# Softmax sums turned into columns for a small reciprocal, and spread from a line in memory

## The chip, the core and the metric

The kernel runs on one core of a Trainium2 chip. The metric is device time in microseconds, the median of several executions of the whole program: one launch that reads the input and the weights from memory and writes the output back.

## The reference

Two attention layers follow each other on four images of 64 channels and 32 x 32 = 1024 positions. Each layer is a group norm, three projections, softmax attention over the 1024 positions, an output projection and a residual.

```python
def layer(x):                                  # twice, with other weights
    h = group_norm(x, 32 groups, w, b)         # per image, two channels to a group
    q, k, v = h @ Wq + bq, h @ Wk + bk, h @ Wv + bv
    attn = softmax(q @ k.T * 64 ** -0.5)       # 1024 x 1024 per image
    return x + (attn @ v) @ Wo + bo
```

The change concerns the softmax's denominators: for each image and layer 1024 sums, whose reciprocals scale the 64 x 1024 result.

## The kernel before

An image of a layer is a unit; there are eight, 0 to 3 for the first layer and 4 to 7 for the second. The 64 channels of one half of the positions lie in partitions 0 to 63, those of the other half in partitions 64 to 127, so a unit's data are tiles of 128 x 512.

Each engine has its own list of instructions, written out by hand in the order in which it runs them; engines meet through semaphores alone. Three units are in work at once. In turn w of the loop (`for w in range(2, LAST)`, turn 1 written out ahead of it in the same manner) TensorE computes the scores of unit w in eight tiles, multiplies the exponentials with the values of units w-1 and w, and computes scores of unit w+1 for their row maxima, in eight steps that share one PSUM tile, `ps_max`; it also projects q and k of unit w+2 into the bank `ps_scores[0]`, from which tile 6 of the scores has to wait until the projections are read. The other engines follow:

- ACT takes the eight exponentials of unit w, `exp(w, t)`, and copies and norms for the units around it.
- DVE reduces each maximum step, `part(w + 1, m)`, joins the eight, `join`, then makes the low parts of q and k of unit w+2 (`low_front`, `low_back`, from `ps_scores[0]`). Ahead of that it works out the group norm's statistics (`own_stats` to `affine`) of unit w+2; `affine` needs a reciprocal root from POOL.
- POOL takes that root, `root(w + 2)`, first, then adds up the exponentials of unit w in six steps; after the fourth it finishes unit w-1, `finish`: it multiplies the attention result with the spread reciprocals `rden` and adds the residual.
- SP issues most DMAs, in order: the spreading of the reciprocals of unit w-1, the swaps of unit w+2 (`cross`, the halves exchanged), the row of maxima of unit w+1 (`place_rows`), and results.

The denominators of unit w-1 come from TensorE in turn w (`denominators`): 256 columns in each partition, every quarter of the 128 partitions holding 256 of the 1024 sums, each repeated in all 32 rows of its quarter. DVE takes reciprocals of this 128 x 256 tile in two halves, `reciprocal(w - 1, 0)` and `(w - 1, 1)`, between two maxima. Eight DMAs of 32 rows each, six from SP and two from ACT, place them into `rden`, 128 x 512. The last two units finish partly on DVE (`finish_tail`).

Of the kernel before, what the change touches and what calls it, by code (L numbers as in the profile page):

```python
# [6 lines left out]
ACT = mybir.ActivationFunctionType  # L7
# [4 lines left out]
P = 128  # L12
C = P // 2
# [17 lines left out]
def attention_pair(nc, x, layer_params, consts, out):  # L31
# [20 lines left out]
    with ExitStack() as ctx:  # L52
# [47 lines left out]
        pick = sb("pick", [P, 4 * C])  # L100
        quarter_rden = sb("quarter_rden", [P, HALF // 2])
        rden = sb("rden", [P, HALF])

# [59 lines left out]
        attn_copied = sem("attn_copied")  # L163
        quarter_done = sem("quarter_done")
        rden_in = sem("rden_in")
        last_spread = sem("last_spread")
# [27 lines left out]
        def back_hi_of(unit):  # L194
            return (back_hi, unit) if unit else (first_back_hi, 1)

        def pool_adds(unit):
            return POOL_ADDS if unit < LAST - 1 else TAIL_ADDS[unit - LAST + 1]
# [4 lines left out]
        def scores_buffer(unit, t):  # L203
            return ps_scores[t % 2] if unit < LAST else (ps_scores[0], ps_scores[1], ps_max)[t % 3]

        block = ctx.enter_context(nc.Block())

        @block.sync
        def _(sp):
# [19 lines left out]
            def place_rows(u):  # L229
# [3 lines left out]
                for n in range(2):  # L233
                    row = q_row[u % 2][n * C:n * C + 1, :].bitcast(F32).rearrange("p (t n) -> p t n", t=JS)
                    sp.dma_start(row, max_rows[n * JS:(n + 1) * JS, :].bitcast(F32)).then_inc(row_in[u % 2], 16)

            def spread_rden(u):
                sp.wait_ge(quarter_done, 2 * u + 2)
                if u == LAST - 1:
                    sp.wait_ge(tail_normed, 1)  # L240
                elif u:
                    sp.wait_ge(normed, u)
                for n in range(2):
                    for block in (2 * n, 2 * n + 1):
                        for c in range(1 if n and u < LAST - 1 else 2):
                            sp.dma_start(rden[quarter(block), c * HALF // 2:(c + 1) * HALF // 2],
                                         quarter_rden[quarter(2 * n + c), :]).then_inc(rden_in, 16)
# [17 lines left out]
            for w in range(UNITS):  # L265
                if w:
                    spread_rden(w - 1)
                if w + 2 < UNITS:
                    swap_hi(w + 2)
                    swap_lo(w + 2)  # L270
                if w + 1 < UNITS:
                    place_rows(w + 1)
                if w > B:
                    store(w - 1 - B)
# [4 lines left out]
        def _(pool):  # L279
# [35 lines left out]
            def finish(u):  # L315
                a = attn[u % 2]
                pool.wait_ge(rden_in, 128 * (u + 1))
                pool.wait_ge(attn_copied, u + 1)
# [25 lines left out]
        def _(act):  # L344
# [106 lines left out]

            def spread_rden(u):
                act.wait_ge(quarter_done, 2 * u + 2)
                if u:
                    act.wait_ge(normed, u)
                for block in (2, 3):
                    act.dma_start(rden[quarter(block), HALF // 2:HALF],
                                  quarter_rden[quarter(3), :]).then_inc(rden_in, 16)

# [17 lines left out]
            for w in range(UNITS):  # L477
# [11 lines left out]
                if prep:  # L489
                    apply_norm(w + 2)  # L490
                exp(w, 4)
                exp(w, 5)
                if prep:
                    high_front(w + 2)
                    high_back(w + 2)
                if 0 < w < LAST:
                    spread_rden(w - 1)
                if 0 < w < LAST:
# [15 lines left out]
        def _(dve):  # L514
# [99 lines left out]
            def first_add(u):  # L614
                dve.wait_ge(exp_done, TILES * u + 2)
                if u >= 2:
                    dve.wait_ge(den_mm, u - 1)
                dve.tensor_tensor(prob_sum[u % 2][:, :], probs[0][:, :], probs[1][:, :],
                                  ALU.add).then_inc(first_added, 1)

            def reciprocal(u, c):
                cols = slice(c * P, (c + 1) * P)
                sums = ps_misc[:, cols] if u < LAST else ps_max[:, HALF + c * P:HALF + (c + 1) * P]
                if c == 0:
                    dve.wait_ge(den_mm, u + 1)
                    if u:
                        dve.wait_ge(rden_in, 128 * u)
                dve.reciprocal(quarter_rden[:, cols], sums).then_inc(quarter_done, 1)  # L628
# [31 lines left out]
            def finish_tail(u):  # L660
                a, n = attn[u % 2], u - LAST + 3
                dve.wait_ge(rden_in, 128 * (u + 1))
                dve.wait_ge(attn_copied, u + 1)
# [61 lines left out]
            part(2, 4)  # L725
            reciprocal(0, 0)
            part(2, 5)
            reciprocal(0, 1)
            part(2, 6)
            part(2, 7)  # L730
            join(2, neg_max[:, :])
            low_front(3)
# [4 lines left out]
            for w in range(2, LAST):  # L737
# [13 lines left out]
                part(w + 1, 5)  # L751
                reciprocal(w - 1, 0)
                if not prep:
                    part(w + 1, 6)
                reciprocal(w - 1, 1)
                if prep:
                    part(w + 1, 6)
                part(w + 1, 7)
                join(w + 1, neg_max[:, :])
                if prep:  # L760
# [19 lines left out]
        def _(pe):  # L780
# [143 lines left out]
            def spread_last(c):  # L924
                if c == 0:
                    pe.wait_ge(pick_set, 4)
                pe.wait_ge(quarter_done, 2 * LAST + c + 1)
                for k in range(2):
# [110 lines left out]
            values(1, 3)  # L1039
            pe.wait_ge(quarter_done, 2)  # L1040
            turn_max(2)
# [11 lines left out]
            for w in range(2, LAST):  # L1053
# [34 lines left out]
                values(w, 3)  # L1088
                pe.wait_ge(quarter_done, 2 * w)
                turn_max(w + 1)  # L1090
# [22 lines left out]
            scores(LAST, 5)  # L1113
            pe.wait_ge(quarter_done, 2 * LAST)
            values(LAST, 0)
# [70 lines left out]
```

## Time and profile before

| | |
|---|---|
| median of 3 runs | 186.86 us (185.61 to 187.11) |
| profiled execution, first to last instruction | 184.0 us |
| what lies around the span, against the median | 2.9 us |
| granted TensorE clock | 1.00 throughout |
| TensorE busy | 174.6 us, 95% of the span |
| DVE busy | 138.3 us, 75% |
| POOL busy | 121.8 us, 66% |
| ACT busy | 100.4 us, 55% |

The profiled execution's own time is its span; the runs' times include what surrounds the span, and for the profiled one no other time is given. Busy shares are averages over the head, the loop and the tail. Matmuls overlap each other, so a busy TensorE is not one at its peak.

### The profile page before, as it was taken

How to read it: one execution, taken by the hardware profiler on the slowest of the kernel's cores; microseconds unless marked ns; L12 is line 12 of the kernel's file. 1: busy time of each engine (PE TensorE's matmuls, PEld its weight loads, DVE VectorE, ACT ScalarE, POOL GpSimd, SP SyncE). 2: the span in 40 equal slices, each digit the busy share in tenths (PEclk: the TensorE clock that was granted, in tenths of full speed). 3: DMA queues.
4: the chain of work that ended last, by engine and by line, in shares of the span. 5: the costliest groups of instructions: out<-in, count | busy, mean ns of one | idle time of the engine just before them, and what ended most of it. 6: DMA issues, size and time to landing. Idle time of an engine off the chain costs nothing.

```text
span 184.0 us, 3303 instructions
## 1 busy us (share of the span) xinstructions
PE 174.6 (95%) x1223; PEld 93.5 (51%) x1223; DVE 138.3 (75%) x208; ACT 100.4 (55%) x137; POOL 121.8 (66%) x81
## 2 busy tenths in 40 slices
PE   7778899999999999999999999999999999999993
PEld 4435545555525644455535645555535555456661
DVE  2799987779887687859875787769875588386763
ACT  3479367606656376436666476527656554466500
POOL 5265017996799929996699949996799939705000
PEclk9999999999999999999999999999999999999999
DMA  5544100500016000420025000500025100110111
GB/s 154 189 100 98 34 2 0 114 4 2 0 34 142 2 0 14 102 60 0 0 54 122 0 4 20 136 18 0 5 59 115 61 0 21 37 61 7 50 57 57
DMA packets 7103, 8.89 MB, mean 48 GB/s; under 512 B 1656, under 2 KB 4144, under 8 KB 7088
## 3 DMA queue, kind: packets, MB, share of 16 engines
q1 hardware_dynamic: 6080, 7.84, 16.9%
q10 hardware_dynamic: 1008, 0.86, 1.6%
q8 instruction: 9, 0.15, 0.3%
q14 instruction: 6, 0.05, 0.1%
HBM read 1.58 MB, written 1.05 MB: 14 GB/s over the span
## 4 chain that ended last, share of the span: by engine, by line
PE 82%; DVE 13%; DMA 1%; issue 1%; POOL 0%; ACT 0%; DVEq 0%; POOLq 0%
PE ps_attn L887 27%; PE ps_max L817 9%; DVE part_max L588 8%; PE ps_scores L855 8%; PE ps_scores L871 7%; PE ps_scores L857 7%; PE ps_scores L859 7%; PE ps_scores L796 3%; PE ps_misc L804 2%; PE ps_attn L894 2%; PE ps_misc L900 2%; DMA xs<-x_dram 1%; PE ps_misc L894 1%; DVE quarter_rden L628 1%; PE ps_misc L831 1%
## 5 line engine op out<-in xcount | busy, mean ns | idle before, releaser
L313 POOL TENSOR_TENSOR prob_sum<-prob_sum,probs 128x1024 f32<-128x1024 f32 x41 | 97.5, 2377 | 29.0 <-ACT probs L441 16.8
L588 DVE TENSOR_REDUCE part_max<-ps_max 128x2 f32<-128x1024 f32 x60 | 73.4, 1224 | 26.3 <-PE ps_max L818 25.8
L441 ACT ACTIVATE probs<-ps_scores 128x1024 f32<-128x1024 f32 x62 | 61.0, 1025 | 46.1 <-PE ps_scores L872 45.4
L887 PE MATMUL ps_attn<-probs,vals 128*64 128x512 f32 x224 | 54.5, 605 | 0.0
L887 PEld LDWEIGHTS ps_attn<-probs,vals 128*64 128x64 f32 x224 | 13.5, 136 | 27.8 <-issue 19.2
L871 PE MATMUL ps_scores<-q_row,ones_r 64*128 64x512 f32 x62 | 24.5, 396 | 0.5 <-ACT q_row L423 0.5
L872 PE MATMUL ps_scores<-q_row,ones_r 64*128 64x512 f32 x62 | 24.6, 396 | 0.0
L817 PE MATMUL ps_max<-back,front 64*128 64x512 f32 x31 | 13.9, 449 | 2.3 <-DVE part_max L588 1.4
L817 PE MATMUL ps_max<-cross,front 64*128 64x512 f32 x29 | 14.6, 505 | 0.3 <-DVE part_max L588 0.3
L818 PE MATMUL ps_max<-cross,back 64*128 64x512 f32 x29 | 14.6, 505 | 0.0
L818 PE MATMUL ps_max<-front,back 64*128 64x512 f32 x31 | 14.0, 450 | 0.0
L628 DVE RECIPROCAL quarter_rden<-ps_misc 128x128 f32<-128x128 f32 x14 | 12.6, 930 | 1.1 <-PE ps_misc L900 1.1
L871 PEld LDWEIGHTS ps_scores<-q_row,ones_r 64*128 64x128 f32 x62 | 11.4, 184 | 3.2 <-issue 0.7
L856 PE MATMUL ps_scores<-back,cross 64*128 64x512 f32 x31 | 12.9, 418 | 0.0
L294 POOL TENSOR_TENSOR rstd<-var_eps,minus_half 128x1 f32<-128x1 f32 x8 | 4.4, 549 | 12.9 <-DVE var_eps L543 12.9
L855 PE MATMUL ps_scores<-front,back 64*128 64x512 f32 x31 | 12.9, 415 | 0.0
L855 PE MATMUL ps_scores<-front,cross 64*128 64x512 f32 x31 | 12.4, 399 | 0.0
L856 PE MATMUL ps_scores<-back,front 64*128 64x512 f32 x31 | 12.4, 399 | 0.0
L860 PE MATMUL ps_scores<-back,cross 64*128 64x512 f32 x31 | 12.1, 392 | 0.0
L859 PE MATMUL ps_scores<-front,back 64*128 64x512 f32 x31 | 12.1, 391 | 0.0
L860 PE MATMUL ps_scores<-back,front 64*128 64x512 f32 x31 | 12.1, 390 | 0.0
L859 PE MATMUL ps_scores<-front,cross 64*128 64x512 f32 x31 | 12.1, 390 | 0.0
(157 smaller groups left out, 365.7 us busy)
## 6 DMA issues: line engine op xcount, KB each, us to landing
cross<-front SPq DMA_DIRECT2D x16, 128.0 KB, 2.3
cross<-back SPq DMA_DIRECT2D x16, 128.0 KB, 2.3
rden<-quarter_rden SPq DMA_DIRECT2D x44, 32.0 KB, 1.8
xs<-x_dram SPq DMA_DIRECT2D x4, 256.0 KB, 4.6
out_dram<-xs SPq DMA_DIRECT2D x3, 256.0 KB, 2.0
rden<-quarter_rden ACTq DMA_DIRECT2D x12, 32.0 KB, 1.9
q_row<-max_rows SPq DMA_DIRECT2D x14, 2.0 KB
layer<-layers_dram SPq DMA_DIRECT2D x1, 194.5 KB, 2.7
```

What stands on the lines that cost most here:

```text
L313: pool.tensor_tensor(total[:, :], total[:, :], probs[t][:, :], ALU.add).then_inc(added, 1)
L441: act.activation(probs[t][:, :], scores_buffer(u, t)[:, :], ACT.Exp, scale=SCALE).then_inc(exp_done, 1)
L588: dve.tensor_reduce(part_max[u % 2][:, at:at + 2 * JS + 1:2 * JS], ps[:, :].rearrange("p (g n) -> p g n", g=2), AX.X, ALU.max, negate=True ...
L817: pe.matmul(ps[:, HI], f[top, tile], (x if crossed else g)[top, HI], start=True, stop=True)
L818: pe.matmul(ps[:, LO], g[low, tile], (x if crossed else f)[low, HI], start=True, stop=True).then_inc(max_mm, 1)
L855: pe.matmul(left, key_top[top, hi], front_u[top, HI], start=True, stop=False)
L856: pe.matmul(right, key_low[low, hi], back_u[low, HI], start=True, stop=False)
L859: pe.matmul(left, key_top[top, lo], front_u[top, HI], start=False, stop=False)
L860: pe.matmul(right, key_low[low, lo], back_u[low, HI], start=False, stop=False)
L871: pe.matmul(left, ones_r[top, :], row[top, :], start=False, stop=True)
L872: pe.matmul(right, ones_r[low, :], row[low, :], start=False, stop=True).then_inc(scores_mm, 1)
L887: mm = pe.matmul(ps_attn[half * C:(half + 1) * C, :], v, probs[t][:, cols], start=(t == 0), stop=(t == TILES - 1))
```

## The change

For units 0 to 4 the way from sums to spread reciprocals is another one. ACT copies the 128 x 256 sums from PSUM into `quarter_den` (`copy_den`, between the fifth and the sixth exp). Four DMAs from SP each read one row of that, 256 sums of one quarter, and lay them out as 8 in each of 32 partitions (`fold_den`), so that `den_cols` is 128 x 8 with all 1024 sums once. DVE takes one reciprocal of that, `fold`, behind its eighth maximum and ahead of the join. SP stores the 128 x 8 result as a line of 1024 numbers in memory, waits for the store, and loads the line's halves back with two DMAs that each repeat 512 numbers into 64 partitions (`unfold_rden`). TensorE waits for ACT's copy instead of DVE's reciprocals before it writes the PSUM tile again. Units 5, 6 and 7 keep the large reciprocals; for unit 5 the two DMAs that ACT issued are now issued by SP.

```diff
+        def folds(unit):
+            return unit < LAST - 2
+
+        def rden_count(unit):
+            return 32 * min(unit + 1, LAST - 2) + 128 * max(unit + 3 - LAST, 0)
+
+        def den_read(unit):
+            return (den_copied, unit + 1) if folds(unit) else (quarter_done, 2 * (unit - LAST + 3))
...
+        rden_line = nc.dram_tensor("rden_line", (P, TILES), F32, kind="Internal").ap()
...
+            def fold_den(u):
+                sp.wait_ge(den_copied, u + 1)
+                for q in range(4):
+                    row = quarter_den[q * QUARTER:q * QUARTER + 1, :].rearrange("p (i e) -> p i e", e=TILES)
+                    sp.dma_start(den_cols[quarter(q), :], row).then_inc(den_folded, 16)
+
+            def unfold_rden(u):
+                sp.wait_ge(fold_done, u + 1)
+                if u:
+                    sp.wait_ge(rden_in, rden_count(u - 1))
+                sp.dma_start(rden_line, rden_cols[:, :]).then_inc(rden_stored, 16)
+                sp.wait_ge(rden_stored, 16 * (u + 1))
+                if u:
+                    sp.wait_ge(normed, u)
+                for n in range(2):
+                    line = rden_line[n * C:(n + 1) * C, :].rearrange("p e -> (p e)").unsqueeze(0).broadcast_to([C, HALF])
+                    sp.dma_start(rden[n * C:(n + 1) * C, :], line).then_inc(rden_in, 16)
+
             def spread_rden(u):
-                sp.wait_ge(quarter_done, 2 * u + 2)
+                sp.wait_ge(*den_read(u))
...
                     for block in (2 * n, 2 * n + 1):
-                        for c in range(1 if n and u < LAST - 1 else 2):
+                        for c in range(2):
...
             for w in range(UNITS):
-                if w:
+                if w and folds(w - 1):
+                    fold_den(w - 1)
+                    unfold_rden(w - 1)
+                elif w:
                     spread_rden(w - 1)
...
-            def spread_rden(u):
-                act.wait_ge(quarter_done, 2 * u + 2)
+            def copy_den(u):
+                act.wait_ge(den_mm, u + 1)
                 if u:
-                    act.wait_ge(normed, u)
-                for block in (2, 3):
-                    act.dma_start(rden[quarter(block), HALF // 2:HALF],
-                                  quarter_rden[quarter(3), :]).then_inc(rden_in, 16)
+                    act.wait_ge(den_folded, 64 * u)
+                act.activation(quarter_den[:, :], ps_misc[:, 0:HALF // 2], ACT.Copy).then_inc(den_copied, 1)
...
                 exp(w, 4)
+                if 0 < w and folds(w - 1):
+                    copy_den(w - 1)
                 exp(w, 5)
...
-                if 0 < w < LAST:
-                    spread_rden(w - 1)
...
+            def fold(u):
+                dve.wait_ge(den_folded, 64 * (u + 1))
+                if u:
+                    dve.wait_ge(rden_stored, 16 * u)
+                dve.reciprocal(rden_cols[:, :], den_cols[:, :]).then_inc(fold_done, 1)
...
                 part(w + 1, 5)
-                reciprocal(w - 1, 0)
-                if not prep:
-                    part(w + 1, 6)
-                reciprocal(w - 1, 1)
-                if prep:
-                    part(w + 1, 6)
+                if not folds(w - 1):
+                    reciprocal(w - 1, 0)
+                part(w + 1, 6)
+                if not folds(w - 1):
+                    reciprocal(w - 1, 1)
                 part(w + 1, 7)
+                if folds(w - 1):
+                    fold(w - 1)
                 join(w + 1, neg_max[:, :])
...
-                pe.wait_ge(quarter_done, 2 * w)
+                pe.wait_ge(*den_read(w - 1))
                 turn_max(w + 1)
```

On DVE, from the group norm's gain to the low parts in a turn of the loop, this is the order before (`part_max` are the maxima, `neg_max` is the join):

```order
L554 TENSOR_SCALAR gain<-rstd,layer 128x1 [waits rstd_ready]
L556 TENSOR_SCALAR shift<-mean_gain,rstd,layer 128x1 [waits stat_step]
L588 TENSOR_REDUCE part_max<-ps_max 128x2 [waits max_mm] x2
L628 RECIPROCAL quarter_rden<-ps_misc 128x128 [waits rden_in,den_mm]
L628 RECIPROCAL quarter_rden<-ps_misc 128x128
L588 TENSOR_REDUCE part_max<-ps_max 128x2 [waits max_mm] x2
L611 TENSOR_REDUCE neg_max<-part_max 128x8 [waits max_turned,max_done]
L572 SCALAR_TENSOR_TENSOR front<-ps_scores,layer,front 128x512 [waits front_hi]
L579 SCALAR_TENSOR_TENSOR back<-ps_scores,back_bias,back 128x512 [waits back_hi]
```

And this is the same place after the change:

```order
L591 TENSOR_SCALAR gain<-rstd,layer 128x1 [waits rstd_ready]
L593 TENSOR_SCALAR shift<-mean_gain,rstd,layer 128x1 [waits stat_step]
L625 TENSOR_REDUCE part_max<-ps_max 128x2 [waits max_mm] x4
L662 RECIPROCAL rden_cols<-den_cols 128x8 [waits rden_stored,den_folded]
L648 TENSOR_REDUCE neg_max<-part_max 128x8 [waits max_turned,max_done]
L609 SCALAR_TENSOR_TENSOR front<-ps_scores,layer,front 128x512 [waits front_hi]
L616 SCALAR_TENSOR_TENSOR back<-ps_scores,back_bias,back 128x512 [waits back_hi]
```

The two large reciprocals between the maxima are gone, and a small one that waits for four DMAs stands between the last maximum and the join.

On SP, one turn of the loop before:

```order
L246 DMA rden<-quarter_rden 32x256 [waits normed,quarter_done]
L246 DMA rden<-quarter_rden 32x256 x5
L218 DMA cross<-front 64x512 [waits front_hi]
L220 DMA cross<-back 64x512 [waits back_hi]
L225 DMA cross<-front 64x512 [waits front_lo]
L227 DMA cross<-back 64x512 [waits back_lo]
L235 DMA q_row<-max_rows 1x4x128 [waits max_staged]
L235 DMA q_row<-max_rows 1x4x128
```

And after the change:

```order
L259 DMA den_cols<-quarter_den 32x1x8 [waits den_copied]
L259 DMA den_cols<-quarter_den 32x1x8 x3
L265 DMA rden_line<-rden_cols 128x8 [waits rden_in,fold_done]
L271 DMA rden<-rden_line 64x512 [waits normed,rden_stored]
L271 DMA rden<-rden_line 64x512
L236 DMA cross<-front 64x512 [waits front_hi]
L238 DMA cross<-back 64x512 [waits back_hi]
L243 DMA cross<-front 64x512 [waits front_lo]
L245 DMA cross<-back 64x512 [waits back_lo]
L253 DMA q_row<-max_rows 1x4x128 [waits max_staged]
L253 DMA q_row<-max_rows 1x4x128
```

Six issues with one wait ahead of them have become seven with three waits, one of them for a DMA that the same queue has issued, and the swaps and rows stand behind all of them.

## Rows read from the trace of the kernel before

**Rows 1.** Turn 3: its length, then busy us of PE, PEld, DVE, ACT, POOL.
```profile
81.74:102.21 20.47, 20.47 (x143) 10.64 (x141) 15.92 (x24) 11.84 (x15) 17.26 (x10) 1.00 0.17 39
```

**Rows 2.** Timeline of DVE, turn 3: start, duration, instruction, idle before and releaser.
```profile
90.09 1.76 DVE L628 RECIPROCAL quarter_rden<-ps_misc 128x128 f32<-128x128 f32 x2
...
94.13 1.23 DVE L588 TENSOR_REDUCE part_max<-ps_max 128x2 f32<-128x1024 f32 x1 [1.02 <-PE ps_max L818]
95.39 0.17 DVE L611 TENSOR_REDUCE neg_max<-part_max 128x8 f32<-128x16 f32 x1
...
96.14 0.74 DVE L579 SCALAR_TENSOR_TENSOR back<-ps_scores,back_bias,back 128x512 fp32r<-128x512 f32 x1
```

**Rows 3.** Timeline of TensorE, turns 1, 3, 4 and the start of 7.
```profile
52.53 0.50 PE L817 MATMUL ps_max<-cross,front 64*128 64x512 f32 x1 [0.32 <-DVE part_max L588]
...
97.29 0.39 PE L855 MATMUL ps_scores<-front,back 64*128 64x512 f32 x1
...
103.26 0.39 PE L871 MATMUL ps_scores<-q_row,ones_r 64*128 64x512 f32 x1
...
108.88 0.50 PE L817 MATMUL ps_max<-cross,front 64*128 64x512 f32 x1
...
161.81 0.39 PE L871 MATMUL ps_scores<-q_row,ones_r 64*128 64x512 f32 x1
```

**Rows 4.** Instructions on the tile q_row: duration in ns (shortest, median, longest).
```profile
L421 ACT ACTIVATE q_row<-ps_misc x1: 492/492/492, 19.0 to 19.0; 128x384 fp32r<-128x384 f32 x1
L423 ACT ACTIVATE q_row<-ps_attn x1: 277/277/277, 20.9 to 20.9; 128x128 fp32r<-128x128 f32 x1
```

**Rows 5.** Timeline of ACT: fifth exp of turn 1 (with the sixth) and of turn 3.
```profile
50.09 1.95 ACT L441 ACTIVATE probs<-ps_scores 128x1024 f32<-128x1024 f32 x2 [1.54 <-PE ps_scores L872]
...
91.65 1.03 ACT L441 ACTIVATE probs<-ps_scores 128x1024 f32<-128x1024 f32 x1 [1.41 <-PE ps_scores L872]
```

**Rows 6.** Timeline of SP's queue, turn 6.
```profile
157.07 1.23 SPq L246 DMA_DIRECT2D rden<-quarter_rden  x2
158.34 1.28 SPq L235 DMA_DIRECT2D q_row<-max_rows  x2
```

**Rows 7.** DMA issues: count, KB each, median us from issue to landing.
```profile
cross<-front SPq DMA_DIRECT2D x16, 128.0 KB, 2.3
...
rden<-quarter_rden SPq DMA_DIRECT2D x44, 32.0 KB, 1.8
...
out_dram<-xs SPq DMA_DIRECT2D x3, 256.0 KB, 2.0
...
out_dram<-xs SPq DMA_DIRECT2D x1, 128.0 KB, 1.7
```

**Rows 8.** Timeline of DVE, turns 2 and 4 and the tail.
```profile
66.36 0.21 DVE L554 TENSOR_SCALAR gain<-rstd,layer 128x1 f32<-128x1 f32 x1
...
107.31 0.20 DVE L554 TENSOR_SCALAR gain<-rstd,layer 128x1 f32<-128x1 f32 x1
...
107.61 1.21 DVE L588 TENSOR_REDUCE part_max<-ps_max 128x2 f32<-128x1024 f32 x1
...
159.56 1.02 DVE L664 TENSOR_TENSOR attn<-attn,rden 128x512 f32<-128x512 f32 x1 [3.87 <-DMA rden<-quarter_rden]
```

**Rows 9.** Line 246 in turn 3 alone: landings of its six copies.
```profile
DMA to landing us min/median/max: 1.8/2.0/2.2
```

**Rows 10.** The chain that ended last: start, duration, what.
```profile
0.74 2.71 DMA xs<-x_dram
```

**Rows 11.** Timeline of POOL, turns 1, 2, 3 and 4.
```profile
56.89 1.29 POOL L319 TENSOR_TENSOR attn<-attn,rden 128x512 f32<-128x512 f32 x1
...
64.35 0.55 POOL L294 TENSOR_TENSOR rstd<-var_eps,minus_half 128x1 f32<-128x1 f32 x1
...
98.59 1.30 POOL L319 TENSOR_TENSOR attn<-attn,rden 128x512 f32<-128x512 f32 x1
...
106.04 0.55 POOL L294 TENSOR_TENSOR rstd<-var_eps,minus_half 128x1 f32<-128x1 f32 x1
```

More of the change, by code:

```diff
@@ L101, in attention_pair @@
         quarter_rden = sb("quarter_rden", [P, HALF // 2])
+        quarter_den = sb("quarter_den", [P, HALF // 2])
+        den_cols = sb("den_cols", [P, TILES])
+        rden_cols = sb("rden_cols", [P, TILES])
         rden = sb("rden", [P, HALF])
@@ L164, in attention_pair @@
         quarter_done = sem("quarter_done")
+        den_copied = sem("den_copied")
+        den_folded = sem("den_folded")
+        fold_done = sem("fold_done")
+        rden_stored = sem("rden_stored")
         rden_in = sem("rden_in")
@@ L316, in finish @@
                 a = attn[u % 2]
-                pool.wait_ge(rden_in, 128 * (u + 1))
+                pool.wait_ge(rden_in, rden_count(u))
                 pool.wait_ge(attn_copied, u + 1)
@@ L626, in reciprocal @@
                     if u:
-                        dve.wait_ge(rden_in, 128 * u)
+                        dve.wait_ge(rden_in, rden_count(u - 1))
                 dve.reciprocal(quarter_rden[:, cols], sums).then_inc(quarter_done, 1)
@@ L661, in finish_tail @@
                 a, n = attn[u % 2], u - LAST + 3
-                dve.wait_ge(rden_in, 128 * (u + 1))
+                dve.wait_ge(rden_in, rden_count(u))
                 dve.wait_ge(attn_copied, u + 1)
@@ L725, in _ @@
             part(2, 4)
-            reciprocal(0, 0)
             part(2, 5)
-            reciprocal(0, 1)
             part(2, 6)
             part(2, 7)
+            fold(0)
             join(2, neg_max[:, :])
@@ L926, in spread_last @@
                     pe.wait_ge(pick_set, 4)
-                pe.wait_ge(quarter_done, 2 * LAST + c + 1)
+                pe.wait_ge(quarter_done, 4 + c + 1)
                 for k in range(2):
@@ L1039, in _ @@
             values(1, 3)
-            pe.wait_ge(quarter_done, 2)
+            pe.wait_ge(*den_read(0))
             turn_max(2)
@@ L1113, in _ @@
             scores(LAST, 5)
-            pe.wait_ge(quarter_done, 2 * LAST)
+            pe.wait_ge(*den_read(LAST - 1))
             values(LAST, 0)
```

## Prediction

> **What bounds the kernel now.** The table above has TensorE busy for 95% of the span. That is an average, so the first view is the busy time in one turn of the loop, turn 3 from 81.74 to 102.21 us: TensorE is busy for all 20.47 us of it, DVE for 15.92, POOL for 17.26, ACT for 11.84 [rows 1]. So in the loop nothing that another engine saves comes back as time, and whatever makes TensorE wait is added in full.
>
> The second view is DVE's own timeline in turn 3 [rows 2]. The two reciprocals take 1.76 us from 90.09, and after them the eighth maximum still waits 1.02 us for TensorE; it starts at 94.13, and the join of the maxima follows at 95.39. The reciprocals lie in a hole that TensorE leaves. What matters is what hangs on the join: DVE makes the low parts of q and k after it and ends them at 96.14 + 0.74 = 96.88, and TensorE starts tile 6 of the scores, which overwrites the bank they are read from, at 97.29 [rows 3]. There is 0.4 us of room, no more.
>
> **What is removed.** Five pairs of large reciprocals, 5 x 1.76 = 8.8 us of DVE. In the loop they hide between two maxima as just said, so I credit nothing; what they would give if that reading were wrong is the rival on the other side, below. ACT also loses two DMA issues per turn, which nobody behind them waited for: nothing either. SP had six issues per turn for this and now has seven.
>
> **What is added, first half: sums into columns.** ACT copies the 128x256 sums out of PSUM. There is no row of this size; 128x128 took 277 ns and 128x384 took 492 [rows 4], so I take 0.385 us, the middle. In turn 3 the fifth exp starts at 91.65 and lasts 1.03 [rows 5], so the copy ends at 92.68 + 0.38 = 93.06. The exp behind it and the two high parts slip by that 0.4 us; DVE's low parts need the high parts, but they now come after something later. Then SP issues four DMAs. Two issues in a row took 1.23 to 1.28 us, up to 0.64 each [rows 6], so the fourth starts at 93.08 + 3 x 0.64 = 95.0. A copy of 32 rows inside SBUF lands 1.8 us after its issue starts [rows 7], which can be checked: the last one of unit 5 starts at 157.07 + 0.62 = 157.69 [rows 6], and DVE, which waits for it, starts at 159.56 [rows 8]. So the columns are there at 96.8. No row shows pieces of 32 bytes; 1.8 is the shortest landing of such a copy and 2.2 the longest in this turn [rows 9]; I take 1.8, the median over all of them.
>
> In the new order the small reciprocal stands behind the eighth maximum and ahead of the join. DVE is free for it at 94.13 + 1.23 = 95.36 and must wait until 96.8. It is one sixteenth as wide as a reciprocal that took about 0.9 us; the join, also eight columns out, took 0.17 [rows 2]; I take 0.2. The join then starts at 97.0 instead of 95.39, the low parts end 1.49 us after the start of the join as before, at 98.5, and tile 6 of the scores starts at about 98.53 instead of 97.29. That is **1.24 us of TensorE waiting in the turn**, in place of 1.76 us of DVE work that cost nothing.
>
> **What is added, second half: the line in memory.** SP can issue the store at 97.03. A store of 128 KB to memory landed after 1.7 us, one of 256 KB after 2.0 [rows 7]; I take 1.75 for these 4 KB, so 98.8. Only then come two loads, starting at 98.8 and 99.45, each of 64 rows of 2 KB. The nearest row is the swap of the same shape, 2.3 us [rows 7]; the first input load, alone on the queue with 256 KB, took 2.71 [rows 10], and the 1.8 of the small copies is the least. I take 2.3: the spread reciprocals are there at 101.75, where POOL took them up at 98.59 before [rows 11]. **POOL waits 3.2 us** in the middle of its adds.
>
> Rows 7 show stores to memory landing no later than copies inside SBUF (1.7 and 2.0 us against 1.8 and 2.3). The Trainium skill, DMA: Bandwidth & Descriptors, section Anatomy of one DMA, speaks against the change here: the semaphore waits until the target has confirmed the last byte, and "This can cause a surprisingly long delay especially when the write target is HBM"; it gives about 2.0 us as the fixed cost. By that figure the store would be 0.25 us later in each turn and the total, as an estimate, about 1.2 us higher than mine.
>
> Who waits for POOL? After the adds it takes the root for the group norm of a later unit: at 106.04 before, now at 109.2, ending at 109.8. DVE comes to that point in order: it used the root at 107.31 and went on with a maximum from 107.61 to 108.82 [rows 8], and TensorE's next maximum starts at 108.88, just behind it [rows 3]. Of POOL's 3.2 us, 0.7 is room between the root's end (106.59) and 107.31; 2.5 us pass through DVE to TensorE. The 1.24 us from the join come before this wait in time and are contained in the 2.5, not added: both count from the same sums on, and the later arrival sets the turn. So each such turn takes **2.5 us more**, 23.0 instead of 20.47.
>
> SP's queue is moved too. The four swaps and the two rows of maxima were issued right behind the six copies; now they stand behind the wait for the store. The second load starts at 99.45, four swaps and two rows follow, the second row starts at 103.3 and lands at 105.1, against 103.26 + 1.24 = 104.5 where TensorE wants it for the next unit's tile 0 [rows 3]. About 0.7 us, hidden in the 2.5 where that applies.
>
> **The sum.** Turn 1: the fifth exp ends at 51.12 [rows 5], and by the same steps the columns are there at 55.25 and the spread at 60.2 instead of 56.89, 3.3 us late. The root had more room here, from 64.90 [rows 11] to 66.36 [rows 8], so 1.85 us reach TensorE. Turns 2, 3 and 4 hand 2.5 each to the next turn: 7.5. Turn 5 has no later root, so only the join (1.24) and the late row (0.7) count: 1.95. In turn 6 the two DMAs that ACT issued for unit 5 go to SP: the rows of unit 7 start at 158.34 + 1.28 = 159.62, the second at 160.26, landing at 162.06 [rows 6], where TensorE took them at 161.81 [rows 3] with its weights a little before: 0.4. DVE's tail from 159.56 on slips by about one microsecond; TensorE has other tiles there, so nothing. Together 1.85 + 7.5 + 1.95 + 0.4 = 11.7 us. Against the profiled execution the span goes from 184.0 to 195.7. The median of the runs, 186.86, lies 2.9 us over that span for what surrounds it, which doesn't change: **198.6 us**.
>
> **The rivals.**
> First, POOL catches up: the landings are shorter, or the root's delay is swallowed by the idle time that POOL had ahead of a unit's first add. Then only the join, the last row and turn 6 count: 5 x 1.24 + 0.7 + 0.4 = 7.3 us, 194.2. Against it: that idle time lies behind the root, not ahead of it.
> Second, the three landings are longer than any copy here. With 2.71 for each of them [rows 10], a turn loses 2.3 us more (0.9 + 0.95 + 0.4): 4.15 + 3 x 4.8 + 4.2 + 0.4 = 23, giving 210. For it: four of the transfers are cut into pieces of 32 bytes. The same page of the Trainium skill, section Specifications, has transfers under 512 bytes done as read-modify-write; it gives no time for that, and no row shows it.
> Third, on the other side, DVE is what TensorE waits for around the reciprocals. In turn 1 TensorE's last maximum waited 0.32 us for DVE [rows 3]; if each of the five turns gives that back and all transfers hide, 1.6 us come off: 185.3. It decides if the columns land before 95.36 and the spread before 98.59, that is 1.4 and 3.2 us sooner than reckoned. With four issues and three landings in line I see no way to it.
> Fourth, the change does not act: the waits are there but fall in room that I can't see, and the time stays at 186.9, within 1%. About 1% is also what a measurement of this kernel can tell from no change, given runs from 185.61 to 187.11.
>
> **How the numbers follow.** The forecast of 198.6 gets 0.64, POOL catching up 0.14, the long landings 0.16, the gain 0.02, no change 0.04. With the shorter value of every landing and issue (0.7 us less per turn) the forecast's own sum is about 8.3 us, 195.2; with 2.2, 2.0 and 2.71 (1.05 more) about 16.8, 203.7. To take in the first rival the range starts at 193.6, and it ends at 204. Slower by over 1%: 0.94; within 1%: 0.04; faster: 0.02.
>
> **What would show it.** In the profile after: DVE idle ahead of a 128x8 reciprocal, released by DMA, for 1.4 us or somewhat more; tile 6 of the scores released by DVE's low part; POOL idle ahead of its multiplication by the spread reciprocals, released by DMA, for 3 to 4 us; DVE idle ahead of the gain, released by POOL's root; turns 2 to 4 at about 23 us, and the last two nearly as long as before. If DVE doesn't wait at the small reciprocal, the landing of the columns was the wrong term; if POOL waits and the turns stay at 20.5, the step from the root to TensorE was.

## The result, and the profile after

The changed kernel takes 203.03 us (median of four runs, 201.78 to 204.75) against 186.82 for the kernel before: a ratio of 1.0879, interval 1.0811 to 1.0948. It is 16.2 us slower; the forecast was 198.6 in a range of 193.6 to 204.0. The profiled execution took 204.75 us with a span of 202.7.

The first view after is the page: busy time by engine, and the shares of the chain that ended last.

```profile
PE 180.7 (89%) x1223; PEld 95.0 (47%) x1223; DVE 134.5 (66%) x203; ACT 101.4 (50%) x142; POOL 125.8 (62%) x81
...
PE 38%; POOL 28%; DVE 14%; issue 13%; ACT 2%; DMA 2%; SPq 1%; POOLq 0%; DVEq 0%; ACTq 0%
```

TensorE no longer bounds the loop alone. A chain through POOL and DVE does, and POOL has 28% of it. The second view is the waits of POOL, DVE and TensorE: total us, times, longest.

```profile
POOL attn L358 <- DMA rden<-rden_line: 21.0, 5, 4.5
...
DVE rden_cols L662 <- DMA den_cols<-quarter_den: 5.6, 5, 1.3
...
DVE gain L591 <- POOL rstd L333: 2.4, 5, 0.6
...
PE ps_max L860 <- DVE part_max L625: 10.1, 12, 1.7
...
PE ps_scores L914 <- DMA q_row<-max_rows: 1.4, 2, 1.0
```

The three new waits stand where they were expected: DVE ahead of the small reciprocal, POOL ahead of its multiplication, DVE ahead of the gain. How they follow one another is read in one turn, from the sums of unit 2 to those of unit 3. The timelines of SP's queue, DVE, POOL and TensorE there, in this order:

```profile
100.03 2.48 SPq L259 DMA_DIRECT2D den_cols<-quarter_den  x4
103.92 0.34 SPq L265 DMA_DIRECT2D rden_line<-rden_cols  x1
105.33 1.14 SPq L271 DMA_DIRECT2D rden<-rden_line  x2
```

```profile
103.68 0.20 DVE L662 RECIPROCAL rden_cols<-den_cols 128x8 f32<-128x8 f32 x1 [1.27 <-DMA den_cols<-quarter_den]
...
104.51 0.74 DVE L616 SCALAR_TENSOR_TENSOR back<-ps_scores,back_bias,back 128x512 fp32r<-128x512 f32 x1
...
114.39 1.22 DVE L625 TENSOR_REDUCE part_max<-ps_max 128x2 f32<-128x1024 f32 x1
115.53 1.90 DVE L655 TENSOR_TENSOR prob_sum<-probs 128x1024 f32<-128x1024 f32 x1
117.87 0.21 DVE L591 TENSOR_SCALAR gain<-rstd,layer 128x1 f32<-128x1 f32 x1 [0.44 <-POOL rstd L333]
```

```profile
108.86 1.28 POOL L358 TENSOR_TENSOR attn<-attn,rden 128x512 f32<-128x512 f32 x1 [4.17 <-DMA rden<-rden_line]
...
111.45 4.90 POOL L352 TENSOR_TENSOR prob_sum<-prob_sum,probs 128x1024 f32<-128x1024 f32 x2
116.30 1.53 POOL L333 TENSOR_TENSOR rstd<-var_eps,minus_half 128x1 f32<-128x1 f32 x1
```

```profile
95.89 0.64 PE L943 MATMUL ps_misc<-prob_sum,ones 128*32 128x256 f32 x8
...
105.36 0.47 PE L898 MATMUL ps_scores<-front,back 64*128 64x512 f32 x1 [0.57 <-issue]
...
119.45 0.50 PE L860 MATMUL ps_max<-cross,front 64*128 64x512 f32 x1 [1.40 <-DVE part_max L625]
...
119.89 0.64 PE L943 MATMUL ps_misc<-prob_sum,ones 128*32 128x256 f32 x8
```

Read them from the sums at 95.89. The columns are there 7.8 us later (103.68), and POOL takes up the spread reciprocals 13.0 us after the sums (108.86); before, it took them up 9.8 us after them (98.59 in [rows 11], with the sums of that unit at 88.83). POOL then runs through its adds, takes the root, and only then can DVE make the gain, at 117.87; the next sums follow 2.0 us behind. Before, the gain at 107.31 [rows 8] also stood 2.0 us ahead of the next sums, at 109.31. Two durations differ from before: the root took 1.53 us instead of 0.55 [rows 11], and DVE's first add (the line above the gain, the first of the adds over a unit's exponentials) 1.90 instead of 1.21. TensorE and DVE before, in order of time:

```profile
88.83 0.64 PE L900 MATMUL ps_misc<-prob_sum,ones 128*32 128x256 f32 x8
...
106.17 1.21 DVE L618 TENSOR_TENSOR prob_sum<-probs 128x1024 f32<-128x1024 f32 x1
...
109.31 0.64 PE L900 MATMUL ps_misc<-prob_sum,ones 128*32 128x256 f32 x8
```

The landings, from the DMA issues (count, KB each, median us from issue to landing):

```profile
rden<-rden_line SPq DMA_DIRECT2D x10, 128.0 KB, 2.9
...
den_cols<-quarter_den SPq DMA_DIRECT2D x20, 1.0 KB, 1.7
rden_line<-rden_cols SPq DMA_DIRECT2D x5, 4.0 KB, 1.4
```

All kernels can be compared by the distance between the sums of one unit and the next (the start of the eight matmuls on `prob_sum` and `ones`). Below, turn w goes from the sums of unit w-1 to those of unit w, and handles the reciprocals of unit w-1; it begins some 7 us later than the turn of the same number in the prediction. Each figure is the difference of two such starts in the profiled execution.

```
turn                      1      2      3      4      5      6    median us  ratio to before
before                  21.31  20.47  20.48  20.46  20.28  15.81   186.82
after                   24.76  24.25  24.00  23.96  23.41  17.36   203.03    1.0879
reciprocal later        28.54  27.32  24.22  24.17  23.47  15.82   210.69    1.1302
constant                22.17  22.20  21.57  21.93  21.49  15.82   192.43    1.0343
both                    27.20  24.89  21.71  22.22  21.70  15.81   201.39    1.0809
first add later         23.75  23.42  23.38  23.45  21.52  15.96   197.63    1.0608
distinct rows           24.31  24.38  23.78  24.01  22.99  15.80   202.93    1.0886
unit 2 alone            21.31  20.48  24.35  20.48  20.28  15.81   189.77    1.0176
unit 4 alone            21.31  20.47  20.48  20.47  23.08  15.81   189.13    1.0164
constant, rows first    21.30  20.47  20.46  20.47  20.28  15.81   186.08    0.9986
```

Turn 6 of the changed kernel is 1.55 us longer than before in this execution alone: TensorE's granted clock was 0.64 and 0.51 in 168 to 172 us, that is near the lower of its two levels (1.2 of 2.4 GHz), after it had waited 1.68 us for a maximum at 166.84. The three other runs had a granted clock of 1.000 and took 201.78 to 203.32 us. So this is set aside below, and the turns of the table, each from one execution, are not expected to add up to the difference of the medians.

### The profile page after: what moved, and what is told of

The parts are those of the page before. It is cut to its first block, busy times and chain, and to the rows that moved or that the text cites. A ratio compares the mean times of both kernels' runs of the same rounds, so it can differ in the third digit from the quotient of the medians.

```text
span 202.7 us, 3301 instructions
## 1 busy us (share of the span) xinstructions
PE 180.7 (89%) x1223; PEld 95.0 (47%) x1223; DVE 134.5 (66%) x203; ACT 101.4 (50%) x142; POOL 125.8 (62%) x81
## 4 chain that ended last, share of the span: by engine, by line
PE 38%; POOL 28%; DVE 14%; issue 13%; ACT 2%; DMA 2%; SPq 1%; POOLq 0%; DVEq 0%; ACTq 0%
POOL prob_sum L352 20%; PE ps_attn L930 10%; DVE part_max L625 8%; PE ps_max L860 4%; PE ps_scores L898 4%; POOL rstd L333 3%; PE ps_scores L914 3%; PE ps_scores L900 3%; PE ps_scores L902 3%; POOL xs L361 3%; POOL attn L358 3%; ACT probs L480 2%; PE ps_attn L937 2%; DVE prob_sum L655 2%; PE ps_misc L943 2%
## 5 line engine op out<-in xcount | busy, mean ns | idle before, releaser
L914 PE MATMUL ps_scores<-q_row,ones_r 64*128 64x512 f32 x62 | 25.3, 408 | 1.9 <-DMA q_row<-max_rows 1.4
L915 PE MATMUL ps_scores<-q_row,ones_r 64*128 64x512 f32 x62 | 25.3, 409 | 0.0
L358 POOL TENSOR_TENSOR attn<-attn,rden 128x512 f32<-128x512 f32 x5 | 6.4, 1275 | 21.0 <-DMA rden<-rden_line 21.0
L860 PE MATMUL ps_max<-back,front 64*128 64x512 f32 x31 | 14.4, 463 | 3.4 <-DVE part_max L625 2.5
L333 POOL TENSOR_TENSOR rstd<-var_eps,minus_half 128x1 f32<-128x1 f32 x8 | 8.4, 1044 | 12.7 <-DVE var_eps L580 12.7
L898 PE MATMUL ps_scores<-front,back 64*128 64x512 f32 x31 | 13.6, 439 | 2.6 <-issue 2.0
L655 DVE TENSOR_TENSOR prob_sum<-probs 128x1024 f32<-128x1024 f32 x8 | 14.7, 1838 | 0.8 <-ACT probs L480 0.8
L559 DVE BATCH_NORM_STATS2 stats<-xs 128x6 f32<-128x512 f32 x8 | 5.5, 691 | 14.4 <-POOL xs L361 11.1
L860 PEld LDWEIGHTS ps_max<-cross,front 64*128 64x128 f32 x29 | 5.4, 187 | 20.0 <-DVE part_max L625 18.7
L861 PE MATMUL ps_max<-front,back 64*128 64x512 f32 x31 | 14.5, 466 | 0.0
L899 PE MATMUL ps_scores<-back,cross 64*128 64x512 f32 x31 | 13.8, 445 | 0.0
L901 PE MATMUL ps_scores<-back,cross 64*128 64x512 f32 x31 | 12.4, 400 | 0.0
L900 PE MATMUL ps_scores<-front,back 64*128 64x512 f32 x31 | 12.4, 399 | 0.0
L902 PE MATMUL ps_scores<-front,back 64*128 64x512 f32 x31 | 12.4, 399 | 0.0
```

Source lines behind the costliest of these rows:

```text
L860: pe.matmul(ps[:, HI], f[top, tile], (x if crossed else g)[top, HI], start=True, stop=True)
L861: pe.matmul(ps[:, LO], g[low, tile], (x if crossed else f)[low, HI], start=True, stop=True).then_inc(max_mm, 1)
L898: pe.matmul(left, key_top[top, hi], front_u[top, HI], start=True, stop=False)
L900: pe.matmul(left, key_top[top, hi], front_u[top, LO], start=False, stop=False)
L902: pe.matmul(left, key_top[top, lo], front_u[top, HI], start=False, stop=False)
L914: pe.matmul(left, ones_r[top, :], row[top, :], start=False, stop=True)
```

## The experiments

The first four ran beside a kernel before of 186.31 us, the others beside one of 186.56.

**1. The small reciprocal behind the low parts.** The join and the low parts of q and k no longer wait for the columns; the reciprocal, and so the store, comes after them.

```diff
-                if folds(w - 1):
-                    fold(w - 1)
                 join(w + 1, neg_max[:, :])
                 if prep:
                     low_front(w + 2)
                     low_back(w + 2)
+                if folds(w - 1):
+                    fold(w - 1)
...
```

> The changed kernel, with the small reciprocal moved behind the low parts of q and k on DVE, so that neither the join nor TensorE waits for the columns; the spread reciprocals come about 0.3 us later per turn. Theory A (the loop: sums, copy, columns, store, loads, POOL's finish, POOL's root, DVE's gain and maximum, TensorE's next sums sets the length of turns 2 to 4): nothing is gained there, 4 x 0.3 us are lost and 1.2 us gained in turn 5, so 203 us, within 1 us of the changed kernel. Rival B (DVE's wait ahead of the join is what costs, POOL's wait is covered): the wait of 1.2 us goes in five turns, so 197 us.

Measured: 210.69 us, ratio 1.1302 (1.1267 to 1.1337). Turns 3 and 4 are 24.2 us, 0.2 longer than in the changed kernel although DVE's wait is gone: as theory A had it, the join wait is contained in the longer path through POOL. In turn 5, where I had expected 1.2 us back, nothing came (23.47 against 23.41). Turns 1 and 2 are 3 to 4 us longer than in the changed kernel, which neither theory had. SP's queue in turns 1 and 3, then TensorE in turn 1 and a window of it (length, busy PE, PEld, DVE, ACT, POOL, granted clock, DMA share, GB/s):

```profile
56.69 0.34 SPq L265 DMA_DIRECT2D rden_line<-rden_cols  x1
60.06 1.15 SPq L271 DMA_DIRECT2D rden<-rden_line  x2
...
111.50 0.33 SPq L265 DMA_DIRECT2D rden_line<-rden_cols  x1
112.91 1.14 SPq L271 DMA_DIRECT2D rden<-rden_line  x2
```

```profile
66.20 0.49 PE L915 MATMUL ps_scores<-q_row,ones_r 64*128 64x512 f32 x1 [3.34 <-DMA q_row<-max_rows]
```

```profile
68.00:70.00 2.00, 1.69 (x6) 0.64 (x8) 1.86 (x9) 1.18 (x2) 1.86 (x2) 0.50 0.01 4
```

The store of 4 KB landed 3.4 us after its issue in turns 1 and 2, where 1.4 is the rule. SP waits for it, so the swaps and the rows of maxima behind it were late, TensorE waited 3.34 us for a row, and its clock then was 0.50 until about 74 us: one delay paid twice. The DMA queues in 55 to 61 us name a neighbour:

```profile
q8 instruction: 1, 0.02, 1.4%
```

One 0.02 MB packet of instructions moved while the store was out. The same stands beside the late store of turn 2 (a packet in 85 to 86 us, the store issued at 84.18). In the changed kernel the packet of that moment was moved after 57.5 us, when the store of turn 1 had landed (the loads were issued at 56.49), and no store was late. That the packet held the store up is argued from this coincidence; no run moved it.

**2. POOL multiplies by a constant.** All transfers are made, but POOL waits for none of them; the kernel leaves out the division by the sums for units 0 to 4.

```diff
-                pool.wait_ge(rden_in, rden_count(u))
+                pool.wait_ge(even_set, 1)
                 pool.wait_ge(attn_copied, u + 1)
-                pool.tensor_tensor(a[:, :], a[:, :], rden[:, :], ALU.mult).then_inc(normed, 1)
+                pool.tensor_tensor(a[:, :], a[:, :], even[:, :], ALU.mult).then_inc(normed, 1)
...
+            pool.memset(even[:, :], 0.001).then_inc(even_set, 1)
...
```

> The changed kernel, but POOL multiplies the results of units 0 to 4 with a constant tile and waits for no loads; all copies, transfers and the small reciprocal stay. Left out: the division by the sums for these units. Theory A: POOL's wait of some 4.2 us goes, and with it the loop; the join's wait stays, so turns of about 21.7 us and 186.8 + 5 x 1.2 + 1 for the late rows = 193.8 us. Rival B: POOL's wait was covered, so 203 us still.

Measured: 192.43 us, ratio 1.0343 (1.0312 to 1.0374). Ten of the sixteen us are gone, so POOL's wait sets the turn; what the join and the row of maxima cost under it is the other six (experiment 8 confirms that nothing else is left).

**3. Both edits together.**

> Both edits before at once: the small reciprocal behind the low parts, and POOL multiplying units 0 to 4 with a constant (the division left out for these units). Theory A: neither wait is left, only the late rows and the two more issues of SP for unit 5, so 187 to 188.5 us, turns of 20.5. Rival B: as with the small reciprocal moved alone, 197 us.

Measured: 201.39 us, ratio 1.0809 (1.0766 to 1.0853). Neither theory had this. TensorE's waits in it:

```profile
PE ps_scores L918 <- DMA q_row<-max_rows: 9.7, 5, 3.0
```

In turns 1 and 2 the store was late again (3.0 us each, with an instruction packet at the same time), TensorE waited 2.98 and 2.78 us for a row, and its granted clock fell to 0.50 after both waits, as in experiment 1. But turns 3 to 5, which none of this touched, took 21.7 to 22.2 us, no less than with the constant alone. I had expected the rows to cost little once the join was free. They take its place instead: SP issues them behind the store's landing, and TensorE waits 1.15 to 1.65 us for them in each of these turns.

**4. DVE's first add behind the root.** The long root and the long first add suggested that the two engines hold each other up. The add is moved behind the gain and one maximum; nothing else changes.

```diff
                 part(w + 1, 3)
-                first_add(w)
                 if prep:
                     affine(w + 2)
                 part(w + 1, 4)
+                first_add(w)
```

> The changed kernel, with DVE's first addition of a unit's exponentials moved behind the group norm's gain and shift and the fifth maximum in turns 2 to 6. In the changed kernel this addition and POOL's root run at the same time and take 1.9 and 1.5 us instead of 1.2 and 0.55. Theory A with that collision in the loop: the root takes 0.55 again, turns 2 to 4 fall from 24.0 to about 23.0, and four times 1.0 us come off: 199 us. Rival C (the root is long for a reason of its own, or isn't in the loop): the root stays at 1.5 or the time stays at 203 us.

Measured: 197.63 us, ratio 1.0608 (1.0572 to 1.0644), 2.7% of the time before less than the changed kernel. The root's line (duration ns: shortest, median, longest), then DVE and POOL in the same turn as above:

```profile
L333 POOL TENSOR_TENSOR rstd<-var_eps,minus_half x8: 543/552/558, 5.5 to 138.5; 128x1 f32<-128x1 f32 x8
```

```profile
115.61 0.22 DVE L591 TENSOR_SCALAR gain<-rstd,layer 128x1 f32<-128x1 f32 x1 [1.27 <-POOL rstd L333]
...
117.05 1.22 DVE L655 TENSOR_TENSOR prob_sum<-probs 128x1024 f32<-128x1024 f32 x1
```

```profile
107.59 1.28 POOL L358 TENSOR_TENSOR attn<-attn,rden 128x512 f32<-128x512 f32 x1 [2.65 <-DMA rden<-rden_line]
...
115.03 0.55 POOL L333 TENSOR_TENSOR rstd<-var_eps,minus_half 128x1 f32<-128x1 f32 x1
```

I had expected 199 us, four times 1.0 less. The gain is 5.4 us, and it is spread otherwise: 1.0, 0.8, 0.6 and 0.5 us in turns 1 to 4, and 1.9 in turn 5, which I had not counted. Root and first add are back at 0.55 and 1.22 us. From the start of POOL's multiplication to the root's it is still 7.44 us, as in the changed kernel (108.86 to 116.30) and before; what shrank is the stretch from the root's start to the gain, from 1.57 to 0.58, that is by 1.0. Turn 3 shrank by only 0.6, because POOL took up the reciprocals 13.35 us after the sums (94.24 to 107.59) where it was 12.97: the ten loads landed after 3.1 us in the median here, against 2.9. No run shows why. Turn 5 falls to 21.52, which is 1.24 over before.

**5. Loads of distinct rows.** Is it the one line, read 64 times, that makes the loads land after 2.9 us?

```diff
-                    line = rden_line[n * C:(n + 1) * C, :].rearrange("p e -> (p e)").unsqueeze(0).broadcast_to([C, HALF])
+                    line = x[0][n * C:(n + 1) * C, :]
```

> The two loads that spread the reciprocals read 64 different rows of 2 KB from the input in memory, where the changed kernel reads one line of 2 KB 64 times over; waits, sizes and order stay. What POOL multiplies by is no reciprocal then, so the sums are left out of the result. Question: why do these loads land after 2.9 us, where the swap of the same shape took 2.3 and I had put 2.3? Theory A, the single line that all 64 rows read is what takes the time: the landing falls to 2.3 to 2.7 us, POOL's wait in the middle of its adds falls from 4.1 by as much, and with five turns the time is 200 to 202. Rival B, it is what any load of 64 rows from memory takes in this place: the landing stays at 2.8 to 3.1 us and the time at 203, within one us.

Measured: 202.93 us, ratio 1.0886 (1.0825 to 1.0947), nothing gained. The landings of the ten loads:

```profile
DMA to landing us min/median/max: 2.5/2.7/3.3
```

At most 0.2 us of the 2.9 belongs to the repeated line: in size rival B. Why such a load lands later than the swap of the same shape (2.3 in [rows 7]) stays open; the first input load took 2.71 [rows 10].

**6. Unit 2 alone.** The unit number decides which form runs; the counts of the semaphores follow, and ACT issues its two copies again for the other units.

```diff
-            return unit < LAST - 2
+            return unit in (2,)
...
```

> Only unit 2 has its sums laid out as columns and its reciprocals spread from memory; all other units keep the two large reciprocals and the copies inside SBUF of the kernel before. Nothing of the computation is left out. Theory A, the price is paid turn by turn, by the chain through the sums, POOL's root and DVE's gain: the one turn that handles unit 2 goes from 20.5 to about 24.0 us as it did among five such turns, the others stay at 20.3 to 20.5, the total is 189.5 to 190.5. Rival B, a good part of the 16 us comes from turns that push each other (late rows of maxima, a POOL that never catches up): alone, the turn would cost 1.2 to 2.5 us and the total 187.5 to 189.

Measured: 189.77 us, ratio 1.0176 (1.0135 to 1.0217). Turn 3 took 24.35 us, all others their time before within 0.02. The price is paid turn by turn; nothing builds up between turns.

**7. Unit 4 alone.** The same edit with 4 in place of 2.

> Only unit 4 has its sums laid out as columns and its reciprocals spread from memory; all others are as in the kernel before. Nothing of the computation is left out. The turn that handles unit 4 has no later root, so by my prediction only the join and the late row of maxima cost time there: 1.95 us, to 188.3. Theory A, the prediction's step holds and the rest that was seen in the changed kernel's last two turns (23.4 us and 17.4 us where 20.3 and 15.8 stood) is DVE's first add running into POOL's adds of this one unit: the first add takes more than 3 us, TensorE's maximum waits 1 to 2 us behind it, the total is 190 to 191. Rival B, the late units suffer from what the earlier turns left behind (POOL late already): then the first add takes about 1.2 us, the turn costs at most 2 us, and the total is 187.5 to 188.5.

Measured: 189.13 us, ratio 1.0164 (1.0105 to 1.0223). Turn 5 took 23.08 us, 2.8 more than before, and turn 6 its old time. DVE, POOL and TensorE there:

```profile
148.16 3.09 DVE L668 TENSOR_TENSOR prob_sum<-probs 128x1024 f32<-128x1024 f32 x1
```

```profile
145.26 4.91 POOL L355 TENSOR_TENSOR prob_sum<-prob_sum,probs 128x1024 f32<-128x1024 f32 x2
```

```profile
152.44 0.50 PE L881 MATMUL ps_max<-cross,front 64*128 64x512 f32 x1 [1.31 <-DVE part_max L638]
```

Theory A: the first add takes over 3 us and TensorE's maximum waits behind it, with no earlier turn to blame. The total lies under A's 190 to 191: that had the long turn 6 of the changed kernel in it, and here the clock stayed at 1.00.

**8. Constant, reciprocal later, and the rows first.** Experiment 3 (which leaves out the division) with the store, SP's wait for it and the loads moved behind the swaps and the rows of maxima.

```diff
                     fold_den(w - 1)
-                    unfold_rden(w - 1)
...
                     place_rows(w + 1)
+                if w and folds(w - 1):
+                    unfold_rden(w - 1)
```

> As the third kernel here (POOL multiplies by a constant, so the division by the sums is left out; the small reciprocal stands behind the low parts), and SP issues the swaps and the rows of maxima of the next unit ahead of the store and the two loads. All transfers and the small reciprocal are still made, but nobody in the loop waits for a landing of theirs. Theory A, the whole loss is three waits (DVE at the join for the columns, POOL for the loads, TensorE for the row of maxima that stands behind the store's landing on SP), and the work itself costs next to nothing: turns of 20.5 to 20.9 us, the total 186.5 to 188.5. Rival B, the added work itself costs, above all ACT's copy and the transfers that run beside the swaps: turns of 21.5 us or more, 190 to 193.

Measured: 186.08 us, ratio 0.9986 (0.9964 to 1.0008), no difference from before, and every turn within 0.02 us of it. SP's queue in it:

```profile
97.93 1.33 SPq L255 DMA_DIRECT2D q_row<-max_rows  x2
99.36 0.38 SPq L267 DMA_DIRECT2D rden_line<-rden_cols  x1
```

ACT's copy, the small reciprocal, the store and all the loads are still there and cost nothing; the 8.8 us of large reciprocals are gone from DVE and bring nothing. The whole loss is waits.

## Why the prediction came out as it did

**What bounds the kernel, and what the removal is worth.** Right. Experiment 8 removes the large reciprocals, waits for nothing in the loop, and is as fast as before: TensorE's turn of 20.47 us is the floor, and the rival in which DVE's 8.8 us come back gave nothing.

**The path from the sums to POOL.** Right to 0.2 us as a whole, though not in its parts. Counted from the sums, the reciprocal was to start after 7.97 us and started after 7.79; the spread was to be there after 12.92 and was taken up after 12.97. Copy (0.37 for 0.385), issues (2.48 for four) and columns (1.7 for 1.8) held. The store landed in 1.4 us where I took 1.75, and the loads in 2.9 where I took 2.3; that these misses cancel is luck. The root, reckoned 20.4 us after the sums, started 20.41 after them.

**The warnings on the landings.** The Trainium skill, page DMA: Bandwidth & Descriptors, section Anatomy of one DMA — SWDGE (gpsimd) path, warns of a long delay where the target is HBM and gives about 2.0 us as the fixed cost. By its heading that section is on DMAs that GpSimd issues, which the prediction did not say; these here are issued by SP, and the trace has 1.4 us for the store. The late stores of experiments 1 and 3 (3.0 to 3.4 us) show that a longer delay can come. The same page of the Trainium skill, section Specifications, has transfers under 512 bytes done as read-modify-write; the pieces of 32 bytes landed in 1.7 us, no later than the larger copies in [rows 9].

**The step that was mis-sized: from the root to the gain.** I let the root keep its 0.55 us and so made the turn 23.0; it was 24.0. The root took 1.53, and that is the whole difference. The reason is that POOL's delay, 3.2 us, pushed its add under DVE's first add, and then its root behind it. Where they overlap, the first add ends 1.08 us after POOL's add does, however early it started: in turn 3 POOL's add ends at 116.35 and the first add at 117.43; with unit 4 alone, 150.17 and 151.25. The root then ends 0.4 us after the first add, at 117.83. Moving the first add (experiment 4) gave both their old times and took 1.0 us out of the way from the root to the gain, and in experiments 2, 3 and 8, where POOL does not wait, all roots took under 0.57 us and all first adds at most 1.22 us. So the overlap as the cause of this 1.0 us is shown. The turn of experiment 4 is still 23.38 and not 23.0, by the later loads told there. A maximum that DVE reads from PSUM lay under the same POOL adds and was not longer (114.39, 1.22 us).

The Trainium skill has a rule for this that I had not weighed: the page SBUF — State Buffer, section SBUF: two separate sides, says that DVE and GpSimd share a pair of ports as an exclusive lock, held for the whole instruction, when DVE reads two inputs from SBUF and GpSimd reads SBUF, and that the other "fully blocks". The trace agrees as far as the 1.08 us go: that is nearly the 1.21 us that the first add takes alone, as if it began only when POOL's add was over. One overlap speaks for a milder form: before, the root (106.04 to 106.59) and the first add (106.17, 1.21 us) overlapped by 0.4 us and neither was longer. That the ports are the cause, and not something else the two share, no run here separates.

**Turn 1** was to cost 1.85 us and cost 3.45: 1.0 of the difference is the same overlap, and 0.6 that POOL took up the reciprocals 13.74 us after the sums (60.62, the sums at 46.88) where the prediction had 13.15. The second load landed after 3.5 us there, not 2.9, again with an instruction packet beside it (57.5 to 58 us); here too the packet as the cause is not shown.

**Turn 5** was to cost 1.95 (join and late row) and cost 3.13. Here the same overlap was larger: the first add took 3.45 us and TensorE waited 1.68 us for the maximum behind it. Without the overlap the turn cost 1.24 (experiment 4), the join alone, just as reckoned: the late row of 0.7 that I added there was not paid, and TensorE waited for no row in it. **Turn 6** was to cost 0.4; it cost 0.15 or nothing where the clock stayed up (15.96 in experiment 4, 15.80 in experiment 5).

**The late row.** I put it at 0.7 us (105.1 against 104.5 makes 0.6) and hidden in the 2.5. In the changed kernel that is right (two waits, 1.4 us in all). Experiment 3 shows it as a bound of its own: take the join's wait and POOL's away and TensorE waits for the row instead, 1.15 us or more in each turn.

**The sum.** By the ratios, the kernel with the first add out of the way is 0.0608 of 186.3 us over before, or 11.3, against 11.7 in the prediction; the overlap adds 0.0271, or 5.1. That 11.3 is so near 11.7 is in part luck: in the profiled execution of experiment 4, the longest of its four, the six turns are 2.44 + 2.95 + 2.90 + 2.99 + 1.24 + 0.15 = 12.7 us over before, each of the first four more than reckoned and the last two less. The range held because it took in 1.05 us more per turn for longer landings. What came was 1.0 us more per turn for another reason, which the prediction put at nothing; that the range still held it is luck, and one of the four runs (204.75) lies outside.

**The rivals.** POOL catching up did not happen: unit 2 alone costs as much as among five (experiment 6). Its time of 194.2 is near what the kernel gives when POOL need not wait (192.43). Landings of 2.71 each did not happen for two of the three. The change did act, and nothing of DVE's freed time came back.

## What to carry to other kernels

Work that an engine does in its idle time costs nothing, as the large reciprocals here; replacing it by a chain of landings costs time if something on another engine waits for the chain's end. Count such a chain from the event that starts it to the first place where the bounding engine feels it, and credit the freed engine only if it is what that engine waits for. When a change delays an engine by a few us, look also at what then runs beside it: instructions of DVE and GpSimd that used to pass each other may lengthen one another. And a wait placed on a queue delays everything issued behind it, here the rows of maxima.

## What the runs showed of the hardware

- DVE's first add (two inputs in SBUF, 128x1024) took 1.21 us alone and 1.90, 3.09 and 3.45 us when it began beside a GpSimd add of 2.4 us, ending 1.08 us after that add each time; a GpSimd root of one column took 1.53 instead of 0.55 behind it.
- A store of 4 KB to memory landed in 1.4 us, and in 3.0 to 3.4 in four cases (turns 1 and 2 of experiments 1 and 3), each with an instruction packet moved while it was out.
- After TensorE had waited 3.34 us, its granted clock was 0.50 for about six us (experiment 1); after 1.31 us (experiment 7) and 1.65 us (turn 4 of experiment 3) it stayed at 1.00, and after 1.68 us it fell to 0.51 in one execution of the changed kernel.
- Ten loads of 64 rows of 2 KB from memory landed in 2.9 us, with distinct rows in 2.7, and in 3.1 in experiment 4, where nothing about them was changed; the swap of that shape inside SBUF, in 2.3 [rows 7].
